# A two-layer graph-attention kernel: layer 2's d scores go through DRAM, leaky moves to ScalarE, and the written-out orders change

## Time and profile before

| | |
|---|---|
| median of 3 runs | 1311.41 us |
| span of the profiled execution | 1309.3 us; its own time is not recorded apart from the span |
| the runs' median less the span | 2.1 us |
| TensorE busy | 1265.7 us, 97% |
| ScalarE busy | 1251.5 us, 96% |
| VectorE busy | 1209.1 us, 92% |
| GpSimd busy | 913.2 us, 70% |
| DMA queue of the kernel | 31.62 MB, 7.7% of 16 engines' span |
| granted TensorE clock | at least 0.9 of full speed in every slice but the last |

### The profile page before, as it was taken

One profiled execution on the slowest core, in us unless ns is written; L12 is line 12 of the kernel. 1 busy time (PEld: TensorE's weight loads), 2 busy tenths in 40 slices (PEclk: granted clock), 3 DMA queues, 4 the chain that ended last, 5 costly groups with the idle time before them and its releaser, 6 DMA issues.

```text
span 1309.3 us, 33375 instructions
## 1 busy us (share of the span) xinstructions
PE 1265.7 (97%) x10511; PEld 918.9 (70%) x10511; DVE 1209.1 (92%) x4401; ACT 1251.5 (96%) x3701; POOL 913.2 (70%) x1106
## 2 busy tenths in 40 slices
PE   5999999999999999999999999999999999999974
PEld 3666677777777777777777777777777777777653
DVE  5789999999999999999999999999999999999987
ACT  5699999999999999999999999999999999999986
POOL 5664776767776767776777776776776676777753
PEclk9999999999999999999999999999999999999998
DMA  6000000000000000000000000000000000000000
GB/s 176 14 1 16 27 16 28 14 28 28 28 16 28 26 16 28 28 16 27 27 16 28 28 25 18 26 16 28 28 28 16 27 16 25 28 28 16 14 13 25
DMA packets 29854, 33.74 MB, mean 26 GB/s; under 512 B 10481, under 2 KB 29681, under 8 KB 29681
## 3 DMA queue, kind: packets, MB, share of 16 engines
q1 hardware_dynamic: 29680, 31.62, 7.7%
HBM read 19.03 MB, written 12.58 MB: 24 GB/s over the span
## 4 chain that ended last, share of the span: by engine, by line
PE 88%; ACT 3%; DVE 3%; POOL 2%; DMA 1%; issue 1%; SPq 1%; POOLq 0%; DVEq 0%; ACTq 0%
PE job L623 27%; PE pt L696 18%; PE job L635 14%; PE unit L670 7%; PE job L718 7%; PE job L764 6%; PE job L611 4%; PE unit L687 3%; PE job L773 2%; ACT p L874 1%; DMA xb<-in_x_dram 1%; PE job L619 1%; POOL prod L1282 1%; ACT pT L884 1%; DVE y L1051 1%
## 5 line engine op out<-in xcount | busy, mean ns | idle before, releaser
L874 ACT ACTIVATE p<-y,min 128x256 f32<-128x256 f32 x768 | 394.1, 539 | 0.9 <-DVE min L1125 0.8
L1119 DVE SCALAR_TENSOR_TENSOR unit<-unit,s,dst 128x256 f32<-128x256 f32 x768 | 335.8, 482 | 14.0 <-issue 1.7
L696 PE MATMUL pt<-ident,p 128*128 128x128 f32 x2304 | 331.5, 275 | 12.3 <-ACT p L874 7.1
L623 PE MATMUL job<-w,h 128*128 128x384 f16 x1728 | 311.1, 326 | 1.8 <-DVE h L1024 1.7
L696 PEld LDWEIGHTS pt<-ident,p 128*128 128x128 f32 x2304 | 268.3, 142 | 42.9 <-ACT p L874 14.0
L1125 DVE CUSTOM_DVE_ANT_0 y<-unit,mask 128x256 f32<-128x256 f32 x768 | 290.5, 414 | 0.0
L1260 POOL TENSOR_SCALAR p<-p,rec 128x256 f32<-128x256 f32 x384 | 178.7, 481 | 123.3 <-DVE rec L1058 122.9
L623 PEld LDWEIGHTS job<-w,h 128*128 128x128 f16 x1728 | 168.6, 98 | 97.3 <-DVE h L1024 2.5
L884 ACT ACTIVATE pT<-pt 128x512 f32<-128x512 f32 x384 | 232.3, 624 | 1.6 <-PE pt L696 1.6
L635 PE MATMUL job<-h,w 128*128 128x256 f16 x1728 | 216.4, 274 | 2.3 <-DVE h L1024 2.1
L830 ACT ACTIVATE p<-y,min 128x256 f32<-128x256 f32 x384 | 191.0, 503 | 13.8 <-PE pt L696 7.9
(11 more groups left out here) (122 smaller groups left out, 2297.2 us busy)
## 6 DMA issues: line engine op xcount, KB each, us to landing
xb<-in_x_dram SPq DMA_DIRECT2D x32, 384.0 KB, 3.2
out_dram<-y SPq DMA_DIRECT2D x31, 384.0 KB, 2.5
pT<-in_w_all_dram SPq DMA_DIRECT2D x4, 576.0 KB, 7.9
adj_raw<-in_adj_dram SPq DMA_DIRECT2D x32, 64.0 KB, 1.9
prod<-in_w_all_dram SPq DMA_DIRECT2D x1, 576.0 KB, 5.4
p<-in_w_all_dram SPq DMA_DIRECT2D x1, 576.0 KB, 6.3
out_dram<-y SPq DMA_DIRECT2D x2, 192.0 KB, 1.9
out_row<-in_bf_dram SPq DMA_DIRECT2D x1, 192.0 KB, 6.2
```

The source lines that it names most:

```text
L623: last = mm(bank[:, 0:H], rows[:, i, c, t * P:(t + 1) * P], w16[:, w, j, c, :], start=n == 0, stop=(c, i, j) == (NC - 1, *TERMS[-1]))
L696: last = nc.tensor.transpose(pt_ps[u % 2][:, (2 * hh + kt) * P:(2 * hh + kt + 1) * P], probs[:, u % 3, hh, kt * P:(kt + 1) * P], ident[:])
L874: last = op(p1[:, u % 3, hh, :], y1[:, u % YB, hh, :], ACT.Exp, bias=min1[:, u, hh:hh + 1], scale=-1.0, accum_out=sum1[:, t, h:h + 1])
L1119: V.scalar_tensor_tensor(leaky[:, hh * T:(hh + 1) * T], bank[:, hh * T:(hh + 1) * T], s8[par][:, t, h:h + 1], dst5[:, c % 2, hh, :], ALU.a ...
```

## The change

- d goes another way: DST_T transposes the fp32 d itself (12 rows), VectorE copies it to `ndT`, SyncE writes it to a DRAM tensor (DST_OUT, 12 KB) and reads it back onto all 128 partitions in three pieces of four heads (DST_IN, 4 KB for each partition, 512 KB each, into two buffers). DST, `pick` and SCALED are gone, and so are the three bf16 parts.
- Leaky is one Prelu activation a head on ScalarE (LEAKY, 12 units of two), from the spread rows into the unit bank, with s times 0.2 as its bias; SCORES1 on VectorE keeps only the mask and minimum passes.
- Q and K of one pair of heads share a job bank (QKP, 18 matmuls) and one VectorE pass evacuates both. V, the copy of HEADS, both parts of PV0, all six PT0 and three of the twelve PT1 (3, 7 and 11) are evacuated by VectorE.
- NORMP0's reciprocal is taken once for two units. The heads' scale is folded into RECIP1 (one small pass more).
- GpSimd takes SKIP_H, two extra passes in ELU_BIAS (the negative and the positive part of the ELU), and FINISH as two products or sums; ELU_RELU is gone. There is one mask a batch, in three buffers.
- The unit banks are handed round in VectorE's order, so that units of layers 1 and 2 alternate, and the pt banks in PE's order.
- The weights' sums, scales and high parts come in another order at the start: all six sums and then all six high parts on ScalarE, ahead of the first exponentials. For Q and K the scales are combined by a square root on GpSimd (ROOT).
- The iteration runs over n = 5 to 29 (25 times), with D = n-3 and E = n-4: layer 1 is at batches n+1, n and n-1, layer 2 at n-2 and n-3. STARTING and ENDING are new. STARTING's matmul work holds, against before, 13 for 10 LN_T0, 18 QKP for 15 Q and 15 K, 15 for 12 QK, 12 for 10 V, 29 for 24 PT0, and no DST. ENDING holds, on ScalarE, 51 EXP1 for 26, 12 for 6 EXP0, 48 LEAKY, 20 for 28 PT1, no PT0 for 6 and 5 for 3 ELU_EXP.

The core of the diff (STARTING, ENDING and small edits are left out):

```diff
+PIECE = 4
+
+LAG = {"J": -4, "K": -3, "L": -2, "P": -1, "A": 0, "B": 1, "C": 2, "D": 3, "E": 4}
 
...
 ORDERS = {
     "PE": steps("""
-        B PV1 0, P QK 0, L LN_T0 0, B PT1 9, B PT1 10, P QK 1, A GATE 1, B PT1 11, P QK 2, L LN_T0 1, P PT0 0,
-        B PV1 1, A DST_T 0, P PT0 1, P PT0 2, B OUT_T 0, A DST 0, B OUT_T 1, L Q 0, L K 0, A DST 1, P PT0 3,
-        L K 1, P PT0 4, P PT0 5, A DST 2, P PV0 0, P PV0 1, L Q 1, A PT1 0, A PT1 1, A DST 3, P OUT0 0,
-        P OUT0 1, A DST 4, A PT1 2, L V 0, A PT1 3, L V 1, A PT1 4, L Q 2, P LN_T1 0, A DST 5, P LN_T1 1,
-        A PT1 5, L K 2, A PT1 6, P HEADS 0, A PT1 7, P HEADS 1, A PT1 8, P GATE 0
+        P LN_T0 1, D PV1 0, A QK 0, B PT0 5, D PT1 9, C DST_T 0, A QK 1, B PV0 1, D PT1 10, A QK 2, P QKP 0,
+        B OUT0 0, B OUT0 1, P QKP 1, P QKP 2, A PT0 0, A PT0 1, P V 0, D PT1 11, P V 1, C PT1 0, C PT1 1, D
+        PV1 1, B LN_T1 0, C PT1 2, B LN_T1 1, A PT0 2, D OUT_T 0, A PT0 3, D OUT_T 1, B HEADS 0, B HEADS 1,
+        A PT0 4, C PT1 3, A PV0 0, C PT1 4, B GATE 0, C PT1 5, C PT1 6, B GATE 1, C PT1 7, L LN_T0 0, C PT1
+        8
     """),
     "ACT": steps("""
-        B PT1 8, B EXP1 10, B EXP1 11, A GATE 0, L LN_T0 0, P EXP0 0, P EXP0 1, B PT1 9, B PT1 10, A GATE 1,
-        B PT1 11, P EXP0 2, L LN_T0 1, P PT0 0, P EXP0 3, P EXP0 4, A SCALED 0, P PT0 1, P EXP0 5, P PT0 2,
-        A SCALED 1, P PT0 3, L Q 0, A EXP1 0, P PT0 4, P PT0 5, A EXP1 1, P PV0 0, A SCALED 2, P PV0 1,
-        B ELU_RELU 0, A EXP1 2, A EXP1 3, L Q 1, A PT1 0, A PT1 1, A SCALED 3, B ELU_EXP 0, A EXP1 4, A PT1 2,
-        A EXP1 5, A PT1 3, A SCALED 4, L V 0, A EXP1 6, L V 1, L Q 2, P LN_T1 0, P LN_T1 1, A PT1 4, A EXP1 7,
-        A PT1 5, A SCALED 5, A PT1 6, A EXP1 8, P HEADS 0, P HEADS 1, A PT1 7, A EXP1 9
+        D EXP1 9, D EXP1 10, D EXP1 11, A EXP0 0, A EXP0 1, A EXP0 2, D PT1 9, D PT1 10, C LEAKY 0, C LEAKY
+        1, C LEAKY 2, C EXP1 0, C EXP1 1, C LEAKY 3, C LEAKY 4, C LEAKY 5, A EXP0 3, A EXP0 4, C LEAKY 6, C
+        EXP1 2, C LEAKY 7, C PT1 0, C PT1 1, C LEAKY 8, B LN_T1 0, C PT1 2, B LN_T1 1, A EXP0 5, C EXP1 3, C
+        EXP1 4, B HEADS 0, C EXP1 5, B HEADS 1, C LEAKY 9, C EXP1 6, C LEAKY 10, C LEAKY 11, C PT1 4, C EXP1
+        7, C PT1 5, B GATE 0, C PT1 6, C EXP1 8, B GATE 1, D ELU_EXP 0, C PT1 8, L LN_T0 0, L LN_T0 1
     """),
     "DVE": steps("""
-        B SCORES1 7, L STATS0 0, C FINISH 0, A LN_T1 0, A LN_T1 1, B SCORES1 8, P K 2, B SCORES1 9, A SKIP_H 0,
-        C FINISH 1, B SCORES1 10, B SCORES1 11, B PV1 0, P SCORES0 0, P SCORES0 1, L LN_T0 0, B RECIP1 0,
-        P SCORES0 2, P NORMP0 0, P SCORES0 3, P NORMP0 1, A SCORE_SUM 0, P NORMP0 2, P SCORES0 4, B PV1 1,
-        L LN_T0 1, A DST_T 0, P SCORES0 5, P NORMP0 3, B OUT_T 0, P NORMP0 4, B OUT_T 1, A SCORES1 0,
-        P NORMP0 5, A SCORES1 1, L K 0, A SCORES1 2, L K 1, A SCORES1 3, P PV0 0, P PV0 1, A SCORES1 4,
-        A SCORES1 5, P OUT0 0, P STATS1 0, P OUT0 1, P STATS1 1, P AGGREGATE1 0, A SCORES1 6
+        P LN_T0 0, P LN_T0 1, D PV1 0, A SCORES0 0, B PT0 5, C DST_T 0, A SCORES0 1, D RECIP1 0, A SCORES0
+        2, B PV0 1, A NORMP0 0, A SCORES0 3, A SCORES0 4, A SCORES0 5, P QKP 0, B OUT0 0, C SCORES1 0, B
+        STATS1 0, C SCORES1 1, C SCORES1 2, P QKP 1, B OUT0 1, C SCORES1 3, B STATS1 1, A PT0 0, B
+        AGGREGATE1 0, C SCORES1 4, A NORMP0 1, P V 0, D PT1 11, A PT0 1, P QKP 2, P V 1, C SCORES1 5, L
+        STATS0 0, D PV1 1, B LN_T1 0, A PT0 2, B LN_T1 1, A PT0 3, A NORMP0 2, D OUT_T 0, D OUT_T 1, C
+        SCORES1 6, C SCORES1 7, B HEAD_V 0, A PT0 4, B HEAD_V 1, C SCORES1 8, C PT1 3, A PV0 0, C SCORES1 9,
+        C SCORES1 10, C PT1 7, C SCORES1 11, B SCORE_SUM 0
     """),
     "POOL": steps("""
-        L RSTD0 0, L NORM0 0, A SCORE_PROD 0, C OUT_SUM 0, P NORMP0 0, P NORMP0 1, P NORMP0 2, A MASK1 0,
-        P NORMP0 3, P NORMP0 4, P NORMP0 5, A GATES 0, B ELU_BIAS 0, L MASK0 0, P RES_ROW 0, A SKIP 0,
-        P RSTD1 0, P NORM1 0
+        C GATES 0, E OUT_SUM 0, C SKIP 0, A NORMP0 0, A NORMP0 1, A RES_ROW 0, B RSTD1 0, A NORMP0 2, A
+        NORMP0 3, B NORM1 0, B SKIP_H 0, L RSTD0 0, L NORM0 0, A NORMP0 4, D ELU_BIAS 0, B SCORE_PROD 0, A
+        NORMP0 5, D FINISH 0, P MASK 0
     """),
     "SP": steps("""
-        L LOAD_X 0, C STORE 0, L LOAD_ADJ 0
+        D DST_IN 2, P LOAD_X 0, L LOAD_ADJ 0, C DST_OUT 0, E STORE 0, C DST_IN 0, C DST_IN 1
     """),
 }
 
...
-FIRST, LAST = 3, 2
+FIRST = {"PE": 5, "ACT": 5, "DVE": 5, "POOL": 5, "SP": 5}
...
-    for n in range(FIRST, n_batch - LAST):
+    for n in range(FIRST[engine], n_batch - LAST[engine]):
         order += [(step, idx, n - LAG[phase]) for phase, step, idx in ORDERS[engine]]
...
+            def dst_out(b, par, _):
+                _, _, taken, value = job(b, "DST_T")
+                sp.wait_ge(taken, value)
+                if b.ref >= 2:
+                    sp.wait_ge(s_lk, n_lk.after(b.back(2), "LEAKY", 11))
+                sp.dma_start(dst_rows[par], ndT[par][0:H1, :]).then_inc(s_dout, 16)
+
+            def dst_in(b, par, k):
+                rows, landed, _ = spread(b, k)
+                if k == 0:
+                    sp.wait_ge(s_dout, n_dout.after(b, "DST_OUT"))
+                if k >= 2:
+                    sp.wait_ge(s_lk, n_lk.after(b, "LEAKY", PIECE * (k - 2) + 3))
+                elif b.ref >= 1:
+                    sp.wait_ge(s_lk, n_lk.after(b.back(1), "LEAKY", PIECE * (k + 1) + 3))
+                piece = dst_rows[par, PIECE * k:PIECE * (k + 1), :].rearrange("h t -> (h t)")
+                sp.dma_start(rows[:].rearrange("p h t -> p (h t)"), piece.partition_broadcast(P)).then_inc(landed, 16)
...
+            def qk_columns(b, par, p):
+                first_use(b, p, WQ)
+                first_use(b, p, WK)
+                bank, made = bank_free(b, "QKP", p, (("LN_T0", 0), ("LN_T0", 1)) if p == 0 else ())
+                for w in (WQ, WK):
                     n = 0
                     for c in range(NC):
                         for i, j in TERMS:
-                            last = mm(bank[:, 0:T], w16[:, w, i, c, p * P:(p + 1) * P], h16[0][:, j, c, :],
-                                      start=n == 0, stop=n == 3 * NC - 1)
+                            last = mm(bank[:, w * T:(w + 1) * T], w16[:, w, i, c, p * P:(p + 1) * P],
+                                      h16[0][:, j, c, :], start=n == 0, stop=n == 3 * NC - 1)
...
-                for hh in range(2):
-                    last = mm(unit_ps[c % 2][:, hh * T:(hh + 1) * T], pick[:, 2 * c + hh, :], ndT[par][:],
-                              start=True, stop=True)
-                last.then_inc(s_db, 1)
...
-                op(dst5[:, c % 2].rearrange("p h t -> p (h t)"), unit_ps[c % 2][:], ACT.Copy,
-                   scale=ALPHA).then_inc(s_d5, 1)
+            def leaky(b, par, u):
+                c, t = divmod(u, 2)
+                k, at = divmod(2 * c, PIECE)
+                rows, landed, value = spread(b, k)
+                if t == 0:
+                    act.wait_ge(landed, value)
+                if u == 0:
+                    act.wait_ge(s_sd, n_sd.after(b, "SCORE_SUM"))
+                wait_unit_free(act, b, "SCORES1", u)
+                bank = unit(b, "SCORES1", u)[0]
+                for hh in range(2):
+                    h = 2 * c + hh
+                    last = op(bank[:, hh * T:(hh + 1) * T], rows[:, at + hh, :], ACT.Prelu,
+                              bias=s8[par][:, t, h:h + 1], scale=ALPHA, alpha=1.0 / ALPHA)
+                last.then_inc(s_lk, 1)
 
...
+            def elu_exp(b, par, _):
...
+                op(o1m[:, rows, :], o1m[:, rows, :], ACT.Exp, bias=one[:]).then_inc(s_oe, 1)
...
+            def qk_columns(b, par, p):
+                bank, taken = made(b, "QKP", p)
+                V.scalar_tensor_tensor(qkT[par][:, p, :, :], bank[:].rearrange("p (w t) -> p w t", w=2), post_qk[:],
+                                       bqk_c[:, :, p:p + 1].broadcast_to([P, 2, T]),
+                                       ALU.mult, ALU.add).then_inc(taken, 1)
...
+            def normp0(b, par, p):
+                dve.wait_ge(s_e0, n_e0.after(b, "EXP0", 2 * p + 1))
+                V.reciprocal(rec0[:, 2 * p:2 * p + 2, :], sum0[:, 2 * p:2 * p + 2, :]).then_inc(s_rec0, 1)
 
             def pv0(b, par, i):
-                dve.wait_ge(s_hi0, n_hi0.after(b, "PV0", i))
-                bank, _, taken, _ = job(b, "PV0", i)
+                bank, taken = made(b, "PV0", i)
                 p, n = HALVES[i][0], len(HALVES[i])
                 low, high = [c16[:, k, p:p + n, :].rearrange("p c t -> p (c t)") for k in (1, 0)]
+                V.tensor_copy(high, bank[:, 0:n * T]).then_inc(s_c16, 1)
+                dve.wait_ge(s_c16, n_c16.after(b, "PV0", i))
...
-                    V.scalar_tensor_tensor(leaky[:, hh * T:(hh + 1) * T], bank[:, hh * T:(hh + 1) * T],
-                                           s8[par][:, t, h:h + 1], dst5[:, c % 2, hh, :],
```

(49 more changed lines are left out.)

688 lines of the change are left out of this document (329 added, 359 removed).

## The result

The changed kernel takes 1399.6 us (median of 4 runs, 1397.9 to 1401.1) against 1311.6 for the kernel before on the same chip: ratio 1.067, 95% interval 1.065 to 1.068. It is 88 us slower, where 36 us faster were forecast. The profiled execution has a span of 1396.0 us, 123 more than the 1273 of the sum. Split at the starts of PV1 0 on TensorE, the first step of an iteration that is easy to find, the start is 201.5 us (forecast 195), 25 iterations take 1034.7 (941) and the end 159.7 (137). So 94 of the 123 us are in the iteration: 41.39 us and not 37.63.

A forecast was written before the change was run, and what follows sets the result against it. TensorE was taken to bound the kernel: start 195, 25 iterations of 37.63 (941) and end 137 sum to 1273 us, with 2.1 about 1275. The TensorE-bound forecast was 1255 to 1285; the range 1256 to 1300.

The forecast's parts named there:

- the SyncE and DMA ring: Iteration: d's trip from DST_T through DRAM, LEAKY 0, ScalarE's list, EXP1 9 and PT1 9 takes 36.8 us, covered by TensorE's 37.63.
- With GpSimd at 89% this is what is late next: Iteration: GpSimd's sum is 33.5 us, at worst 36.4, below 37.6; its last steps are late next if anything is.
- TensorE, 37.63: Iteration: 38.95 us less 1.32 for the removed DST pieces, if TensorE stays the bound and waits as little as before.
- ScalarE: Iteration: its sum goes from 38.1 to 35.7 us (33.8 to 38.0), with 24 Prelu activations at 0.40 each.
- Rival 1: ScalarE takes over as bound if a Prelu costs nearly 0.49 us; 1285 to 1308 us, chance 0.17.
- rival 3: Prelu is outside the exp and tanh table; 16 table loads, 20 us an iteration, about 1750 us, chance 0.02.
- Rival 2: Slower DRAM round trip of d, DST_OUT plus DST_IN 0 at 8.0 us or more instead of 5.6; 1337 us, chance 0.08.
- the ring's 6.5 us: Iteration: transposes and copy about 0.7 us, DST_OUT priced 1.9 to 2.5, and DST_IN 0 at 3.7.
- Rival 4: No change: new waits, for instance for GpSimd, replace TensorE's 1.32 us; needs 1.45 us an iteration, chance 0.03.
- My slower rival: Rival 2, headed "Slower" in the prediction: the DRAM round trip, 1337 us, chance 0.08.
- The end: After the iterations: ScalarE's sum 121.4 us, 12.3 behind the last PT evacuation and 3 for waits, 137 (130 to 144).
- The start: Before the iterations: 177.1 us plus 15.2 of TensorE work plus 3 for a later first projection, mostly made up: 195 (190 to 200).

The follow-up runs named there:

- e12: The changed kernel with only the store of the output moved behind the two reads of d on the DMA queue: 1380.6 us.
- e11: The changed kernel with MASK ahead of FINISH and the store behind the reads of d, the row sum keeping its single buffer: 1324.5 us.
- e7: The changed kernel with the row sum in the batch's own skip buffer, MASK ahead of FINISH, and the store behind both reads of d: 1323.7 us.
- e13: e7 with the same moves in ENDING too, each store behind the first reads of d and MASK ahead of FINISH: 1318.1 us.
- e3: The changed kernel with the row sum in the batch's own skip buffer and MASK ahead of FINISH: 1401.3 us.
- e15: e13 with, at the start, HIGH_W 0 and 1 ahead of the last two weight sums and LOW_W 0 and 1 ahead of bias and score rows: 1318.3 us.

## Why the prediction was wrong

- **The failed step** is the claim on the SyncE and DMA ring, 36.8 us and covered by 0.8. I led the ring from ScalarE's EXP1 9 over PT1 9 to DST_T. DST_T was in time (619.22, against the copy's 621.64). The ring closes by another way and takes 41.3 us: from LEAKY 0 to ELU_EXP on ScalarE, FINISH, MASK, GATES and OUT_SUM on GpSimd, the store and the read behind it on the DMA queue. Two sentences let it through. "it only needs OUT_SUM, second on GpSimd's list, and it is issued while DST_OUT is under way": OUT_SUM is second in the list, but the list itself was late, by FINISH and MASK, so the store waited 1.4 us, and the read stood behind it. Moving the store alone (e12) gave 19 us. And of GpSimd's last steps, "for which TensorE has its other steps": the last step is MASK, and SCORES0 0, which waits for it, is the first thing of VectorE's list that it holds, with QK 1, QK 2 and the copy of d behind it. That is the mask ring, 40.7 us, just under the other; moving MASK as well (e11) gave 56 us more.
- **"With GpSimd at 89% this is what is late next"** named the right engine and gave it no price. Its work sum of 33.5 was right (33.2 busy an iteration here, 33.0 in e7). A sum under the period says nothing of a ring in which 4.6 us are GpSimd's (FINISH and MASK in e12) and 36.1 lie on other engines.
- **TensorE, 37.63**: without the rings it is 38.33, 0.7 more (18 us in 25 iterations). Start to next start, in eight iterations of e7 against ten of before, the DST pieces gave 1.43 (I took 1.32 off), but this came back: 0.38 behind OUT_T (the second one takes 0.70 to HEADS 0, 0.33 before; in it is the wait of 0.21 for h), 0.21 in PT0 and PT1 (0.13 of it in front of QK 2, 0.66 against 0.53), 0.15 in PV0 (1.01 and 1.88 apart against 2.74 for the three together in the kernel before), 0.09 in DST_T (0.31 against 0.22) and 0.11 in the 384-column projections. QKP gave 0.10 and the rest 0.03. I had bounded DST_T and left the rest as before.
- **ScalarE** was right: six LEAKY in 2.47 us are 0.40 each, and 350.3 us busy in 400 are 36.2 an iteration of 41.4 (35.7 forecast). Rival 1 did not come. Neither did rival 3: one table load of 1.28 us stands in the trace, at 0.72. By the Trainium skill ("ScalarE: Activation LUTs", Table sets) a function of another set costs a load at each switch; here exp, tanh and Prelu alternated without one.
- **Rival 2** had the sign and the place, not the mechanism. The trip from DST_OUT to LEAKY 0 was 7.1 us (622.07 to 629.19), under the 8.0 from which I let it decide, and by itself, in e7, 5.5; the forecast was 5.6, and it is 1.4 for the write (I took 1.9) and 4.1 for the read (3.7; 4.8 with the store close to it). The 3.2 us that the prediction works out for the read from the Trainium skill ("DMA: Bandwidth & Descriptors", Anatomy of one DMA) come from a fit for DMAs issued by GpSimd; SyncE issues these. Two of my numbers there were off without weight: 192 KB are a fifth of two DST_INs and not a seventh, and the ring's 6.5 us took DST_OUT at 2.1, rival 2 at 1.9.
- **Rival 4** was the nearest: waits in place of TensorE's 1.32 us, with GpSimd in them. I gave it 1.45 us an iteration and a chance of 0.03; the waits came to 3.8 above the forecast (41.39 - 37.63). My slower rival had one cause and one price, and no rival had a ring through three lists.
- **The end**, 137, was 159.7. ScalarE's sum of 121.4 was 125.9; the waits were 34 us and not 15, the term that was mis-sized. ScalarE's own longest are 7.1 us in front of LEAKY for d's rows, 7.0 once for the ELU's negative part from GpSimd and 6.1 for masked scores, in a dependent chain of the last batches, at a granted clock of 0.86. Two of the queue's and the mask's ties are in ENDING too: with both mended, e13 has an end of 155.4 against e7's 158.3. Which wait sets the rest I have not traced. Of the end before, the prediction gives VectorE 72.4 us and ScalarE 63.2; the trace has 66.3 and 66.0 busy.
- **The start**, 195, was 201.5. The added work was right: from the first projection to PV1 0 it is 173.8 us against 158.1 before, 15.7 more (15.2 forecast). The first projection came at 27.73, 8.7 later than before (some 7 forecast). What failed is "most of that is made up": behind its first projection TensorE before had 6.1 us of idle time, and 18.4 in the whole start, not 30, so there was little to make it up in. Between runs that leave STARTING as it is the start lies at 199.4 to 203.7.
- With the rings cut and ENDING mended the layout gives 1318, not 1275. Of the 44 us of span between them (1317.2 against 1273), 21 are the iteration (38.49), 18 the end (155.4) and 5 the start (199.5).

## What to carry to other kernels

In a kernel whose queues are ordered by hand, go through each list and ask of each step that waits for another engine what stands behind it; the DMA queue is such a list too, and a store that waits in front of a read that someone needs costs its wait; its transfer costs too (0.7 us here), in front of the read or close behind it. Sum each ring through all lists it passes, not through the data's path alone, and distrust a margin of 0.8 us in 37. When removing the largest wait changes nothing, look whether the same wait has come back one step later or on another queue, and whether a small wait stands further down the same list: here 0.6 us in front of FINISH said that taking away the 5 us before it would bring nothing. Of the two moves one alone gave nothing, the other 19 us, and both together 75.

## What the runs showed of the hardware

A small VectorE pass ran as long as GpSimd's beside it. RECIP1's second pass (128x24, SBUF to SBUF) takes 864 to 876 ns, median 868, in all 10 of its executions in the stretch of the changed kernel, and 318 to 331 in e3. In the changed kernel it falls into a TENSOR_TENSOR of GpSimd and ends with it:

```profile
622.97 0.87 DVE L1207 TENSOR_SCALAR rec<-rec,post 128x24 f32<-128x24 f32 x1
621.98 1.83 POOL L1404 TENSOR_TENSOR o1m<-o,xskip 128x768 f32<-128x768 f32 x1
```

In e3 and e7 a TENSOR_SCALAR of GpSimd runs beside it, and it isn't held up. Nor is every pass of VectorE: the RECIPROCAL just before it, of the same 128x24, takes 0.28 to 0.29 us beside the same TENSOR_TENSOR. At the start, e15 moved two other passes against GpSimd's row sum. The copy of 2x128 at L990 takes 1.65 us beside it in e13, ending 0.08 us behind it, and 0.21 in e15, with nothing beside it. The pass at L981 does the opposite; e13, then e15, where the row sum runs from 25.08 to 26.88:

```profile
21.75 0.18 DVE L981 TENSOR_SCALAR gat_b_row<-gat_b_row 128x32 f32<-128x32 f32 x1
25.23 1.68 DVE L981 TENSOR_SCALAR gat_b_row<-gat_b_row 128x32 f32<-128x32 f32 x1
```

The 0.55 us of RECIP1 lie in front of SCORES0 2, inside the mask ring. That GpSimd's TENSOR_TENSOR holds such a pass until it ends fits all of these; why some passes are held and others are not, no run here shows.
